# Attention over 4 x 1024 tokens in the last stage: value product by query rows with a ones column, one projection for f and g, scores on halves of TensorE's rows

## The reference

```python
f = jnp.einsum('bhwc,cd->bhwd', inputs, Wq) + bq      # d = 16
g = jnp.einsum('bhwc,cd->bhwd', inputs, Wk) + bk      # d = 16
h = jnp.einsum('bhwc,cd->bhwd', inputs, Wv) + bv      # d = 128
s = jnp.einsum('bnd,bmd->bnm', f, g)
beta = jax.nn.softmax(s, axis=-1)
o = jnp.einsum('bnm,bmc->bnc', beta, h)
return gamma * o + inputs
```

## Time and profile before

| | before |
|---|---|
| median of 3 runs | 471.91 us |
| profiled execution, its own time | 472.0 us |
| its span | 470.2 us |
| PE / DVE / ACT / POOL busy | 384.3 / 366.8 / 306.0 / 251.5 us |
| mean granted TensorE clock | 0.917 |
| last stage, 330.8 us to the end: PE / DVE / ACT / POOL busy | 112.2 / 119.8 / 91.3 / 58.9 us of 139.4 |

### The profile page before, as it was taken

How to read it: one execution, slowest core, us unless ns; L and a number is a source line. 1 busy time by engine, 2 the same in 40 slices (tenths; PEclk the granted TensorE clock), 3 DMA queues, 4 the chain that set the end, 5 groups by cost and what they waited for, 6 DMA issues and landing times. The chain is left out here.

```text
span 470.2 us, 12980 instructions
## 1 busy us (share of the span) xinstructions
PE 384.3 (82%) x4916; PEld 211.4 (45%) x4916; DVE 366.8 (78%) x894; ACT 306.0 (65%) x488; POOL 251.5 (53%) x302
## 2 busy tenths in 40 slices
PE   0436699999999999986697999999777998989684
PEld 0223456666666666665352555554323242333241
DVE  6965679999999999986464666663589989999896
ACT  2634689999999999996232333332487867768561
POOL 4753467766776777669377334430003747737510
PEclk9855889999999999997598999999959998998988
DMA  8300000000000000000000000000000001010011
GB/s 284 109 0 5 2 1 3 0 0 0 0 0 0 0 0 0 0 1 3 0 1 1 2 0 0 1 1 1 1 0 1 0 0 47 1 46 0 0 46 45
DMA packets 4804, 7.09 MB, mean 15 GB/s; under 512 B 1543, under 2 KB 2344, under 8 KB 4648
## 3 DMA queue, kind: packets, MB, share of 16 engines
q1 hardware_dynamic: 3536, 5.25, 3.2%
q10 hardware_dynamic: 1240, 1.46, 0.9%
HBM read 4.61 MB, written 2.10 MB: 14 GB/s over the span
## 5 line engine op out<-in xcount | busy, mean ns | idle before, releaser
L1189 POOL TENSOR_TENSOR el<-e,eh 128x1024 f16<-128x1024 f32 x24 | 51.0, 2125 | 56.3 <-DVE eh L1394 56.3
L1075 POOL TENSOR_TENSOR p_lo<-e_buf,p_hi 128x1024 f16<-128x1024 f32 x32 | 68.1, 2129 | 0.6 <-ACT p_hi L906 0.6
L906 ACT ACTIVATE k_t<-ps 32x512 f16<-32x512 f16 x64 | 37.7, 588 | 21.3 <-DVE q_t L877 18.9
L1463 ACT ACTIVATE e_sum<-ps,mq 128x1024 f16<-128x1024 f32 x32 | 35.6, 1113 | 17.9 <-DVE mq L1365 17.9
L313 PE MATMUL ps<-y_t,fc_w 128*128 128x512 f16 x192 | 47.1, 390 | 0.0
L1235 PE MATMUL ps<-eh,val 128*128 128x512 f16 x128 | 34.5, 394 | 8.9 <-POOL el L1189 5.9
L865 DVE TENSOR_REDUCE ps<-ps 128x16 f32<-128x1024 f32 x32 | 39.5, 1233 | 3.0 <-PE ps L693 2.1
L689 PE MATMUL ps<-mask,identb 128*128 (+1 forms) x128 | 39.8, 393 | 2.1 <-DVE k_t L638 1.1
L700 PE MATMUL ps<-ident,q_rows 128*128 128x128 f16 x256 | 26.3, 227 | 18.5 <-POOL k_rows L1061 17.5
L1449 ACT ACTIVATE e<-ps 128x1024 f32<-128x1024 f32 x32 | 32.6, 1019 | 12.4 <-PE ps L1297 12.4
L1404 DVE TENSOR_REDUCE mx<-ps 128x1 f32<-128x1024 f32 x32 | 38.8, 1213 | 0.8 <-PE ps L1313 0.8
(11 more groups left out here) (155 smaller groups left out, 990.5 us busy)
## 6 DMA issues: line engine op xcount, KB each, us to landing
x_all<-in_x SPq DMA_DIRECT2D x8, 256.0 KB, 6.9
out<-ob SPq DMA_DIRECT2D x8, 256.0 KB, 2.1
mask_f<-in_mask ACTq DMA_DIRECT2D x1, 1024.0 KB, 9.4
fc_w<-in_fc_w SPq DMA_DIRECT2D x1, 512.0 KB, 9.6
fc_w<-in_fc_w SPq DMA_DIRECT2D x1, 256.0 KB, 8.7
qkv_w<-in_qkv_w ACTq DMA_DIRECT2D x1, 192.0 KB
proj_w<-in_proj_w ACTq DMA_DIRECT2D x1, 64.0 KB
ident<-in_ident SPq DMA_DIRECT2D x1, 64.0 KB, 8.5
```

The source lines that it names most:

```text
L906: return act.activation(out, in_, ACT.Copy)
L1075: pool.tensor_tensor(p_lo[:, u], e_buf[:, u], p_hi[:, u], ALU.subtract).then_inc(plo_done, 1)
L1189: eng.tensor_tensor(el[:, key % H_BUFS, :], e4[:, key % E_BUFS, :], eh[:, key % H_BUFS, :], ALU.subtract).then_inc(el_done, 1)
L1463: act.activation(e_sum[:, m % 2, :], two(s_bank(m - 1, cur)), ACT.Exp, bias=mq[:, m - 1:m], scale=1.0, accum_out=den[:, v, m - 1:m]).then_ ...
```

## The change

The last stage is rewritten; nothing else is, but that one more constant is loaded (bv, spread over 128 rows) and other pads are set.

1. **Value product by query rows.** `values` holds a 128 x 128 block of `eh` or `el` as weights and streams `val` (129 columns): 24 matmuls a tile in place of 6. The output lies by tokens, eight query blocks in three PSUM banks. A 129th column of `val` holds ones (times VSCALE), so the denominators come out with the product. The pass of `e_sum`, `mq`, the turning of the reciprocals and `r_rows` go. `finish` takes the reciprocal, times gamma, and one operation per query block gives the output; `turn_x` and `residual` turn x itself to tokens.
2. **f and g in one projection**, 128 rows (`xr`: f above, g below). Its halves are swapped into `yr` by two DMAs within the chip for each 512 tokens.
3. **Scores on row halves.** Each score matmul is 64 rows deep, key or query columns 0 to 511 on rows 0 to 63 and 512 to 1023 on rows 64 to 127, in different banks. The maxima are no longer part of the 128 rows: two more 64-row matmuls with `mconst` and `mrows` add them.
4. **Schedule.** One loop over T, 32 tiles in all. The scores of the first pass are written AHEAD = 10 tiles before the second pass needs them, into one pair of banks (two for the first ten), the second pass has one pair, the value product three banks, and one bank, AUX, serves projections, the turned x and turned maxima in turn, each waiting for the reader of the one before. The cast `eh` moves from VectorE to ScalarE; `el` goes to GpSimd, in the last batch every other one to VectorE.

```diff
+        mh = sb("mh", [128, 2, BT, 128], F16)
+        mconst = sb("mconst", [128, 128], F16)
+        val = sb("val", [128, 2, 2, BT, DIM + 4], F16)
...
-        E_BUFS, H_BUFS = 4, 3
-        VSCALE = 16.0
+        E_BUFS, H_BUFS, LAG, AHEAD = 3, 4, 2, 10
+        TILES = B * BT
...
+            fgh = tmp("fgh", [128, 2, 512], F16)
+            xr = tmp("xr", [128, 3, NB], F16)
+            yr = tmp("yr", [128, 3, NB], F16)
+            mrows = tmp("mrows", [128, 2, NB], F16)
...
+            S4, ST4, PV4, AUX = 0, 2, 4, 7
+            pv4 = ps[:, PV4:PV4 + 3, 0:3 * (DIM + 4)].rearrange("p k (n d) -> p k n d", n=3)
...
+            def by_vector(key):
+                return key >= TILES - BT and key % 2 == 1
...
+            def maxima_of_step(T):
+                if T % BT == 0:
+                    tiles = (T + AHEAD, T + AHEAD + 1)
+                elif T % BT == 1:
+                    tiles = ()
+                else:
+                    tiles = (T + AHEAD,)
+                return [k for k in tiles if k < TILES]
...
+                def scores(k):
+                    b, n, bank = k // BT, k % BT, s_bank(k)
...
+                    if k < AHEAD:
+                        wait(pe, max4_done, k - 1)
+                    else:
+                        pe.wait_ge(max4_done, k - 1 if k == AHEAD else k)
+                    cols = slice(128 * n, 128 * n + 128)
+                    pe.matmul(ps[:, bank, :], xr[0:64, b % 3, cols], yr[0:64, b % 3, 0:512], start=True, stop=True)
+                    pe.matmul(ps[:, bank + 1, :], yr[64:128, b % 3, cols], xr[64:128, b % 3, 512:1024], start=True,
+                              stop=True).then_inc(s4_done, 1)
...
+                def scores_turned(T):
+                    b, n = T // BT, T % BT
+                    if n == 0:
+                        pe.wait_ge(mrow_ready, b + 1)
+                    wait(pe, exp4_done, T)
+                    cols = slice(128 * n, 128 * n + 128)
+                    pe.matmul(ps[:, ST4, :], yr[0:64, b % 3, cols], xr[0:64, b % 3, 0:512], start=True, stop=False,
+                              skip_group_check=True)
+                    pe.matmul(ps[:, ST4 + 1, :], xr[64:128, b % 3, cols], yr[64:128, b % 3, 512:1024], start=True,
+                              stop=False, skip_group_check=True)
+                    pe.matmul(ps[:, ST4, :], mconst[0:64, :], mrows[0:64, b % 2, 0:512], start=False, stop=True,
+                              skip_group_check=True)
+                    pe.matmul(ps[:, ST4 + 1, :], mconst[64:128, :], mrows[64:128, b % 2, 512:1024], start=False,
+                              stop=True, skip_group_check=True).then_inc(st4_done, 1)
...
+                def values(T):
+                    b, m = T // BT, T % BT
                     if m == 0:
+                        pe.wait_ge(v4_ready, 2 * b + 2)
+                    pe.wait_ge(eh_done, T + 1)
+                    def term(j, i, n, weights, part, first, last):
+                        return pe.matmul(pv4[:, j, i, 0:DIM + 1], weights[:, T % H_BUFS, 128 * n:128 * n + 128],
+                                         val[:, b % 2, part, m, 0:DIM + 1], start=first, stop=last,
                                          skip_group_check=True)
+                    if m < BT - 1:
+                        for j in range(3):
+                            if m == 0:
+                                wait(pe, o_ready, 3 * (b - 1) + j + 1)
+                                if b == 0 and j == 0:
+                                    pe.wait_ge(max4_done, AHEAD)
+                            for i, n in enumerate(blocks(j)):
+                                term(j, i, n, eh, 0, m == 0 and i == 0, False)
+                                term(j, i, n, eh, 1, False, False)
+                        wait_low(pe, T)
+                        for j in range(3):
+                            for i, n in enumerate(blocks(j)):
+                                last = term(j, i, n, el, 0, False, False)
+                        last.then_inc(pv4_done, 1)
+                    else:
+                        wait_low(pe, T)
+                        for j in range(3):
+                            for i, n in enumerate(blocks(j)):
+                                term(j, i, n, eh, 0, False, False)
+                                term(j, i, n, eh, 1, False, False)
+                                last = term(j, i, n, el, 0, False, True)
+                            last.then_inc(pvb_done if j < 2 else pv4_done, 1)
...
+                for T in range(TILES + LAG):
+                    b, n = T // BT, T % BT
+                    if T < TILES:
+                        scores_turned(T)
+                        for k in maxima_of_step(T)[:1]:
+                            scores(k)
+                        if n == 7 and b + 1 < B:
+                            pe.wait_ge(v4_ready, 2 * b + 4)
+                            turn_maxima(b + 1)
+                    if T >= LAG:
+                        values(T - LAG)
+                    if T < TILES:
+                        for k in maxima_of_step(T)[1:]:
+                            scores(k)
+                        if n == 0:
+                            if b == 0:
+                                pe.wait_ge(v4_ready, 2)
+                            else:
                                 pe.wait_ge(mrow_ready, b + 1)
+                            turn_x(b, 0)
+                        if n == 1:
+                            pe.wait_ge(xg_ready, 2 * b + 1)
+                            turn_x(b, 1)
+                        if n == 2 and b + 2 < B:
+                            pe.wait_ge(xg_ready, 2 * b + 2)
+                            project_fg(b + 2, 0)
+                        if n == 3 and b + 2 < B:
+                            pe.wait_ge(fg_ready, fg_count(b + 2, 0))
+                            project_fg(b + 2, 1)
+                        if n == 4 and b + 1 < B:
+                            if b + 2 < B:
+                                pe.wait_ge(fg_ready, fg_count(b + 2, 1))
+                            else:
+                                pe.wait_ge(xg_ready, 2 * b + 2)
+                            project_v(b + 1, 0)
+                        if n == 5 and b + 1 < B:
+                            pe.wait_ge(v4_ready, 2 * b + 3)
+                            project_v(b + 1, 1)
...
+                def finish(b, j):
+                    u, n = b % 2, blocks(j)
+                    if j < 2:
+                        dve.wait_ge(pvb_done, 2 * b + j + 1)
+                    else:
+                        dve.wait_ge(pv4_done, b * BT + BT)
+                    wait(dve, o_ready, 3 * b + j)
+                    dve.reciprocal(rec4[:, n[0]:n[-1] + 1], pv4[:, j, 0:len(n), DIM]).then_inc(den_done, 1)
+                    dve.wait_ge(den_done, 3 * b + j + 1)
+                    dve.tensor_scalar(rg[:, n[0]:n[-1] + 1], rec4[:, n[0]:n[-1] + 1], cols[:, 1:2], None, ALU.mult)\
+                        .then_inc(rec4_done, 1)
+                    if j == 0:
+                        dve.wait_ge(xg_ready, 2 * b + 2)
+                        if b >= 2:
+                            dve.wait_ge(stored[u], 48)
+                    dve.wait_ge(rec4_done, 3 * b + j + 1)
+                    for i, k in enumerate(n):
+                        last = dve.scalar_tensor_tensor(out=ob[:, u, k, :], in0=pv4[:, j, i, 0:DIM],
+                                                        scalar=rg[:, k:k + 1], in1=xg[:, u, k, :], op0=ALU.mult,
+                                                        op1=ALU.add)
+                    last.then_inc(o_ready, 1)
...
+                for T in range(TILES + LAG):
+                    b, n = T // BT, T % BT
+                    if n == 7 and b + 1 < B:
+                        maxima_turned(b + 1)
+                    for k in maxima_of_step(T):
+                        maximum(k)
+                    if b < B:
+                        if n == 1:
+                            residual(b, 0)
+                        if n == 2:
+                            residual(b, 1)
+                        if n in (3, 4) and b + 2 < B:
+                            rows_of(b + 2, n - 3)
+                        if n in (5, 6) and b + 1 < B:
+                            low_values(b + 1, n - 5)
+                        if by_vector(T):
+                            dve.wait_ge(eh_done, T + 1)
+                            wait(dve, pv4_done, T - H_BUFS + 1)
+                            dve.tensor_tensor(el[:, T % H_BUFS, :], e4[:, T % E_BUFS, :], eh[:, T % H_BUFS, :],
+                                              ALU.subtract).then_inc(el_last, 1)
+                    if n == 1 and b >= 1:
+                        for j in range(3):
+                            finish(b - 1, j)
...
+                for T in range(TILES):
+                    b, n = T // BT, T % BT
+                    act.wait_ge(st4_done, T + 1)
+                    wait_low(act, T - E_BUFS)
```

(27 more changed lines are left out.)

454 lines of the change are left out of this document (175 added, 279 removed).

## The result

The changed kernel takes **483.34 us** (median of 4 runs, 482.01 to 484.14) beside 471.67 of the kernel before: ratio 1.0244, 95% interval 1.0222 to 1.0266. It is slower by 11.7 us, and the prediction (465.2, range 457 to 479) is wrong in sign and size. The profiled execution has a span of 481.5 us.

What follows compares the result with a forecast made beforehand. VectorE was taken to bound the kernel before, TensorE after the change. Ahead of the loop and batches 0 to 3, 352.6 + 29.1 + 29.4 + 23.9 + 28.4 = 463.4 us of span, with 1.8 outside it 465.2; range 457 to 479.

Steps and rivals of the forecast that it cites:

- 1.3, 1.3 and 1.0, 3.6 us in all: VectorE's output operations for the three value groups of a batch, each with reciprocal, product and 128-column operations.
- step 2 of batch 1: TensorE waits 0.5 us for outputs and 1.5 more for `residual`: 2.35 + 2.0 + 0.86 = 5.2 us.
- step 0: First step of batch 1 on TensorE: 2.35 + second scores 0.35 + turning x 0.9 = 3.6 us.
- The clock rival: TensorE's clock falls at each batch turn, staying down two steps, some 3 us a batch lost: 474; chance 0.17.
- 3.0 + 3.0 + 2.75: First three steps of batch 3; then ScalarE bounds at 2.16 a step; batch to the end 28.4 us.
- At nothing I cost: smaller memsets: GpSimd's smaller memsets in the MLP stage, taken to lie under work that waits for other things: no gain.
- Ahead of the loop: Projections, first maxima, their turn and value projection before the loop: transposed scores start at 352.6 us, before 356.6.
- batches 0 to 2: The loop's first three batches on TensorE: 29.1, 29.4 and 23.9 us.
- weights that show: Rival: value weights don't hide behind 129 columns, unhidden 1.0 us a step and 490; chance 0.06.
- full overlap of the pairs: Score matmuls on row halves: 0.215 us a pair of 512 columns if wholly overlapped; 0.25 was taken.
- steps 3 to 5: Batch 1, where the projection waits for exponential, ScalarE's cut and VectorE's rest: 4.15 us each.
- Both rivals on TensorE's forms: Half-height pairs don't overlap: 480.6, chance 0.13; value weights don't hide behind 129 columns: 490, chance 0.06.

Runs made afterwards that it cites:

- e7: The change, with GpSimd's `el` of tiles 7 to 11 cut to 4 of 1024 columns (output lacks these low parts): 474.79 us.
- e8: The change, with reciprocals in PSUM and, from the eleventh tile on, both parts of the maximum written by single-element operations: 469.05 us.
- e9: e8 with VectorE's order changed: second `residual` ahead of the step's maximum, last batch's outputs ahead of `el`: 461.79 us.
- e3: The kernel before, its five pad memsets on GpSimd written as 32-bit words, half as many elements: 465.88 us.
- e6: The change with reciprocals in PSUM, the maximum's low part as two single-element operations, `residual` ahead of the maximum, last outputs ahead of `el`: 467.65 us.
- e4: The change, with useless matmuls in TensorE's waits for the outputs, in batches 1 and 2 that step's scores behind the first value product: 484.3 us.

## Why the prediction was wrong

- **The step that failed** is that of the outputs: "1.3, 1.3 and 1.0, 3.6 us in all" in step 2 of batch 1, for which TensorE was to stand 0.5 us, and with it step 0 at 3.6. I priced each operation from rows where nothing ran beside it. Measured: outputs 6.9 us, TensorE standing 1.73 and 2.17 us for them, step 2 10.05 us for 5.2, step 0 5.2 for 3.6, the low part of the maximum 478 ns on average, 0.22 us where GpSimd is idle. With GpSimd idle the price holds nearly: outputs 4.1 and step 2 5.4 us (e7). Stalls and the clock behind them cost 14.3 us (e8).
- **The sign of it was in the trace before.** The cast `eh` has a mean of 921 ns, 0.69 us where GpSimd stands idle and 1.01 where it is issued inside an `el` (359.08 to 361.20):

```profile
358.31 0.69 DVE L1394 CAST eh<-e 128x1024 f16<-128x1024 f32 x1 [0.63 <-ACT e L1449]
360.74 1.01 DVE L1394 CAST eh<-e 128x1024 f16<-128x1024 f32 x1
359.08 2.12 POOL L1189 TENSOR_TENSOR el<-e,eh 128x1024 f16<-128x1024 f32 x1 [41.53 <-DVE eh L1394]
```

I used neither. The small operations beside it had one element and were not touched, so 0.16 to 0.22 for them was true and could not be carried to two elements. The Trainium skill (GPSIMD Engine Reference, Specifications) says that the SBUF interfaces are shared, with contention for VectorE instructions in a two-port mode or with two SBUF inputs. The Trainium skill (VectorE: DVE Perf Modes, What auto-detection actually checks) gives as the condition of the two-port mode a single source and the destination in SBUF, with outermost extents, those of one left aside, both even or equal. The runs agree in every case tried: two and three elements wait, one element and a PSUM source don't. The reason, shared interfaces, is what the Trainium skill gives; the traces show the wait, of up to 2.1 us for 0.2 us of work.

- **The clock rival** came true in mechanism (0.50 behind each of the three turns) and in sign, at 483 where it gave 474. It was priced for the 2 us of waits of step 2 that I counted, without the stalls that deepen them. Without stalls the clock does not fall in batches 1 and 2 (e8), though TensorE still waits there. So in these batches the clock is a price of the stalls and not a cause beside them.
- **Batch 3**: "3.0 + 3.0 + 2.75" took no account of `el` on VectorE ahead of the outputs. e8 has 32.9 us, e9 with the order changed 27.8, the predicted 27.8. So of its 6.0 us some 5 are the order and less than 1 the stalls.
- **"At nothing I cost: smaller memsets"** is worth 4.4 us on the other side in the traces (e3: 5.0 between the medians). I said they lay under work that waits for other things; GpSimd's timeline names `g_rows` as the releaser of `veps`. Without it the change would, by that, have stood near 488.
- **Ahead of the loop**, 2.2 us late: the eight copies of rows are issued 0.6 us apart on one queue, so the first scores wait 3.31 us, and ScalarE's table load (1.28 us), hidden at 336.73 before, stands in front of the first exponential.
- **Luck and slips.** Even without stalls the sum would have missed: e8 stands 3.9 us over the forecast with 4.4 us of memsets in it that I counted at nothing, so 8 us, of which 2.2 lie ahead of the loop and 5 in the order of batch 3. That batches 0 to 2 of e8 add up to the predicted 82.4 us within 0.3 is in part luck, since batch 0 is 1.6 us under and the other two 0.9 over each. Behind 8.75 us in batch 3 stand four times 2.16 (17.4), not five; the terms given ahead of the loop add up to 351.8, not 352.6; and weights that show at 1.0 us in each of 32 steps would give 497, not 490. None of these decides.
- **Right:** full overlap of the pairs, weights hidden (0.057 us a matmul), steps 3 to 5 at 4.27 for 4.15, the last exponentials 2.0 us apart for 2.16, VectorE relieved. Both rivals on TensorE's forms fell.
- **Not only short operations.** The traces also have VectorE's `el`, with two inputs in SBUF. In the kernel before one of them was issued while GpSimd worked until 448.53, and took 2.17 us instead of 1.22:

```profile
445.58 2.95 POOL L1197 TENSOR_TENSOR ob<-o,xg 128x512 f32<-128x512 f32 x2 [3.66 <-DVE o L1349]
447.44 2.17 DVE L1189 TENSOR_TENSOR el<-e,eh 128x1024 f16<-128x1024 f32 x1
450.32 1.22 DVE L1189 TENSOR_TENSOR el<-e,eh 128x1024 f16<-128x1024 f32 x1
```

And in e9 it is GpSimd that comes second, and its `el` takes 2.69 us instead of 2.13 (the same in e6):

```profile
437.81 1.22 DVE L1502 TENSOR_TENSOR el<-e,eh 128x1024 f16<-128x1024 f32 x1
438.33 2.69 POOL L1552 TENSOR_TENSOR el<-e,eh 128x1024 f16<-128x1024 f32 x1 [3.77 <-ACT eh L1544]
```

- **Open:** how the 14.3 us divide between the stalls and the clock. The 2.8 us of e4 don't tell it: they belong to batch 3, whose waits come mostly from VectorE's order.

The best version, e9, beats the kernel before by 2.0% (461.79), and the kernel before with short memsets (465.88) by some 4 us, each against the same kernel before: the idea of the change is worth that much once its small operations are kept out of GpSimd's way and VectorE's order is changed.

## What to carry to other kernels

Price an operation by rows in which its neighbours run as they will run: a spread in the durations of one shape (0.69 and 1.01 us of the same cast) is a sign that another engine may have a hand in it. Where GpSimd streams, keep VectorE's short operations off the SBUF-to-SBUF forms of more than one element, above all where TensorE waits behind them; a PSUM source (0.22 us) or two single elements (0.33 us together) cost little. When one operation is freed look at the next in the queue before judging, since a wait moves on to the next that qualifies, and an operation with a steady short time may only be standing behind one that waits for it.
